# Three-block expert dispatch, spaced merges, and one layer norm moved to ScalarE

## The reference

```python
x = x + attn0(LN(x))        # q, k, v projected, each normed with gain and bias; softmax(k q^T) v + input
x = x + recur(LN(x), ctx)   # r_t = 0.9 r_(t-1) + ctx_t^2 along the sequence; LN(x) * r_t
x = x + switch(LN(x))       # top-1 of 8 experts, 256 -> 1024 -> 256 with gelu; capacity 1024 tokens, else passed by
x = x + attn1(LN(x))        # 16 heads of 16 features; q and k normed by head; softmax; projection
x = x + cross(LN(x), ctx)   # token against itself and 256 context rows, softmax
x = x + moe(LN(x))          # top-2 of 8 experts, 256 -> 256 -> 256 with relu, weighted by the raw gate scores

def moe(x, gate_w, gate_b, w1, b1, w2, b2):
    topk_s, topk_i = top_k(x @ gate_w + gate_b, 2)
    comb = zeros.at[token, topk_i].add(topk_s)
    eo = relu(x @ w1[e] + b1[e]) @ w2[e] + b2[e]      # for every expert e
    return sum_e comb[:, e] * eo[e]
```

## Time and profile before

| what | value |
|---|---|
| median of three runs | 2872.43 us |
| profiled execution | 2876.24 us, span 2874.5 us |
| granted TensorE clock, mean | 0.926 of full speed |
| stage one / switch experts | 0 to 562 / 562 to 989 us |
| attention pass / cross pass | 989 to 1938 / 1938 to 2419 us |
| expert stage | 2419 to 2874.5 us |

### The profile page before, as it was taken

The page is one execution under the profiler, slowest core; times in us unless marked ns, Lnnn a source line. Parts: engine busy times, 40 slices in busy tenths (PEclk is TensorE's granted clock), DMA queues, the critical chain, the costliest instruction groups (busy, mean ns, idle before and its releaser), DMA issues. The chain is left out here.

```text
span 2874.5 us, 49242 instructions
## 1 busy us (share of the span) xinstructions
PE 2397.5 (83%) x16164; PEld 1881.5 (65%) x16164; DVE 1971.9 (69%) x4760; ACT 1444.4 (50%) x2778; POOL 1335.4 (46%) x1248
## 2 busy tenths in 40 slices
PE   5888888579999579999999999878999885998670
PEld 3666666469999546566565665547888774997560
DVE  4888888556565357878888888745777775765563
ACT  3666666345555247777777777753444341222110
POOL 5777777544443255444344454403656553002545
PEclk9999999889999878999999999889999997999885
DMA  2222212152121000001000010003333343444665
GB/s 69 59 74 59 74 60 63 47 153 95 63 84 40 25 18 30 27 30 31 30 30 30 27 34 23 23 25 127 103 115 117 111 147 118 140 140 152 205 199 157
DMA packets 208168, 226.68 MB, mean 79 GB/s; under 512 B 32254, under 2 KB 194048, under 8 KB 207664
## 3 DMA queue, kind: packets, MB, share of 16 engines
q1 hardware_dynamic: 186352, 177.14, 19.7%
q0 software_dynamic: 20480, 46.39, 5.1%
q10 hardware_dynamic: 1088, 0.00, 0.0%
HBM read 131.99 MB, written 95.49 MB: 79 GB/s over the span
## 5 line engine op out<-in xcount | busy, mean ns | idle before, releaser
L1333 POOL TENSOR_TENSOR f_hm<-f_hm,f_mhalf 128x64 f32<-128x64 f32 x32 | 347.4, 10856 | 2.7
L1513 DVE TENSOR_REDUCE f_nm<-f_raw 128x4 f32<-128x1024 f32 x256 | 312.1, 1219 | 34.0 <-PE f_raw L1634 33.9
L1406 ACT ACTIVATE f_PT<-f_sco 128x1024 f32<-128x1024 f32 x256 | 262.7, 1026 | 81.7 <-PE f_sco L1652 78.7
L2359 POOL DMA_INDIRECT d_pick<-expert_out,e_out_slots x128 | 129.5, 1012 | 319.0 <-DMA expert_out<-d_eo 227.7
L2378 ACT ACTIVATE d_hh<-d_H 128x512 fp32r<-128x512 f32 x78 | 46.7, 598 | 283.9 <-PE d_H L2455 240.7
L1634 PE MATMUL f_raw<-f_k4T,f_q4T 64*128 64x256 f32 x1024 | 140.3, 355 | 37.5 <-DVE f_nm L1513 36.6
L895 ACT ACTIVATE b_hT<-b_H,b_b1r 128x512 f32<-128x512 f32 x128 | 88.3, 690 | 163.5 <-PE b_H L1024 148.5
L1634 PEld LDWEIGHTS f_raw<-f_k4T,f_q4T 64*128 64x128 f32 x1024 | 84.2, 203 | 105.8 <-DVE f_nm L1513 54.3
L1889 POOL DMA_INDIRECT expert_in<-g_xm,e_slots x128 | 130.9, 1023 | 39.7 <-issue 37.0
L1039 PE MATMUL b_O<-b_w2l,b_hTh 128*128 128x256 f32 x512 | 145.8, 285 | 0.0
L1039 PE MATMUL b_O<-b_w2h,b_hTh 128*128 128x256 f32 x512 | 144.8, 283 | 0.0
(11 more groups left out here) (364 smaller groups left out, 7755.6 us busy)
## 6 DMA issues: line engine op xcount, KB each, us to landing
d_xs<-expert_in SPq DMA_DIRECT2D x78, 256.0 KB
expert_out<-d_eo SPq DMA_DIRECT2D x78, 256.0 KB
x_scratch<-a_x SPq DMA_DIRECT2D x64, 256.0 KB, 2.2
b_w<-in_L_ffn_W_dram SPq DMA_DIRECT2D x16, 1024.0 KB
a_x<-in_x_dram SPq DMA_DIRECT2D x32, 256.0 KB
a_cx<-in_ctx_dram SPq DMA_DIRECT2D x32, 256.0 KB
f_x<-x_scratch SPq DMA_DIRECT2D x32, 256.0 KB
f_xr<-x_scratch SPq DMA_DIRECT2D x32, 256.0 KB
```

The lines of the kernel that those rows point to most:

```text
L1333: g.tensor_tensor(hm[b % 2][:, :], hm[b % 2][:, :], mhalf[:, :], ALU.pow).then_inc(hroot, 1)
L1406: s.activation(PT[n % 3][:, t, :, :], heads(SCO), ACT.Exp, scale=float(DH) ** -0.5).then_inc(probs_ready, 1)
L1513: v.tensor_reduce(nm[:, t, g * HG:(g + 1) * HG], heads(RAW), AX.X, ALU.max, negate=True)\
L2359: g.indirect_dma_start(pick[b % GR][:, t, c, :], None, ex.eo_d[k], bass.IndirectOffsetOnAxis(ap=ex.out_slots[:, b, t, c:c + 1], axis=0), b ...
```

## The change

Four edits.

1. In stage one the normalisation of x2 and the row that passes by are made on ScalarE, each as two ACTIVATE (scale and bias per row); the second has a part of its own, "x2 pass". GpSimd's `root4` has five small steps instead of two, since it must give -mean/std and 1 + 1/std as well, and no longer makes the sum itself. The stage's `ORDER` is rewritten.
2. `ORDER` of the attention pass is rewritten.
3. `BLOCKS` is (17, 9, 6). This makes 41 + 25 + 19 = 85 tiles, a third call of `tables` and a third `pad`.
4. GR is 4, and `ready_after` spaces merges 1.5 tiles apart: block 0's 17 after tiles 45, 46, 48, 49, ... 69, block 1's nine after tiles 70, 72, 73, ... 82, block 2's six after the last.

```diff
@@ stage one
-            "in stats", "in norm", "x2 kv", "route logits", "sco scores", "x2 sums", "x2 add", "ln sq", "in T",
-            "x2 stats", "sco exp", "route ranks", "in qk0", "ln scale", "sco prT", "in qk1", "ln kT", "x2 norm",
-            "sco inv", "sco att", "x2 T", "sco stats", "in v", "ln qT")
+            "in stats", "x2 kv", "route logits", "in norm", "sco scores", "x2 sums", "x2 add", "ln sq", "in T",
+            "x2 stats", "sco exp", "route ranks", "in qk0", "ln scale", "sco prT", "ln kT", "in qk1", "x2 norm",
+            "sco inv", "sco att", "ln qT", "x2 T", "sco stats", "x2 pass", "in v")
@@ GpSimd
             def root4(b):
                 pool.wait_ge(var4, b + 1)
-                root(rs4[b % 2][:, :], mv4[b % 2][:, :, 1], T, None, rstd4)
-
-            def passed_by(b):
-                pool.wait_ge(x2n_ready, b + 1)
-                if b >= 3:
-                    pool.wait_ge(x3_stored[b % 3], 16 * (b // 3))
-                g.tensor_tensor(x3[b % 3][:, :, :], x2[b % 3][:, :, :], x2n[b % 2][:, :, :], ALU.add).then_inc(x3_ready, 1)
+                if b >= 2:
+                    pool.wait_ge(x3_ready, b - 1)
+                stand_alone(pool, pool_passed)
+                step(g.tensor_scalar(minus4[:, :], mv4[b % 2][:, :, 0], -1.0, None, ALU.mult))
+                step(g.tensor_scalar(rs4[b % 2][:, :], mv4[b % 2][:, :, 1], EPS, None, ALU.add))
+                step(g.tensor_tensor(rs4[b % 2][:, :], rs4[b % 2][:, :], mhalf[:, 0:T], ALU.pow))
+                step(g.tensor_tensor(nmr4[b % 2][:, :], minus4[:, :], rs4[b % 2][:, :], ALU.mult))
+                g.tensor_scalar(rsp4[b % 2][:, :], rs4[b % 2][:, :], 1.0, None, ALU.add).then_inc(rstd4, 1)
@@ ScalarE
+            def norm4(b):
+                act.wait_ge(rstd4, b + 1)
+                if b >= 2:
+                    wait_full(act, "x2 T", b - 2)
+                for t in range(T):
+                    last = s.activation(x2n[b % 2][:, t, :], x2[b % 3][:, t, :], ACT.Identity,
+                                        bias=nmr4[b % 2][:, t:t + 1], scale=rs4[b % 2][:, t:t + 1])
+                last.then_inc(x2n_ready, 1)
+
+            def passed_by(b):
+                act.wait_ge(rstd4, b + 1)
+                if b >= 3:
+                    act.wait_ge(x3_stored[b % 3], 16 * (b // 3))
...
+                last.then_inc(x3_ready, 1)
@@ attention pass
-            "in stats", "raw 0", "qk scale", "att 0", "raw 1", "att 1", "out o0", "in norm", "out o1", "raw 2",
-            "att 2", "head var", "in normT", "qk gamma", "out oT", "raw 3", "att 3", "in qk0", "qk high", "in qk1",
...
+            "raw 0", "in stats", "att 0", "raw 1", "att 1", "out o0", "in norm", "out o1", "raw 2", "att 2",
+            "qk scale", "head var", "in normT", "qk gamma", "out oT", "att 3", "raw 3", "in qk0", "qk high",
...
+            "att 5", "qk split1", "qk split2", "raw 6", "qk split3", "att 6", "qk split4", "qk split5", "att 7",
+            "raw 7", "raw max1", "qk split7", "qk split6", "raw shift1", "att end")
@@ dispatch and expert stage
-        self.BLOCKS = (B - B // 3, B // 3)
+        self.BLOCKS = (B // 2 + 1, B // 4 + 1, B // 4 - 2)
-    XR, ER, GR = 6, 3, 3
+    XR, ER, GR = 6, 3, 4
-                if k + 1 < len(ex.BLOCKS):
-                    ready_after.append(first[k + 1] + 2 + b * (ex.tiles[k + 1] - 3) // n)
-                else:
-                    ready_after.append(N)
+                after = ready_after[-1] + 1.5 if ready_after else 0
+                ready_after.append(min(N, max(after, first[k] + ex.tiles[k] + 4)))
+        ready_after = [int(m) for m in ready_after]
```

More of the change, by code:

```diff
@@ L156, in phase_a @@
         x2, st4, mv4, rs4 = sbn("x2", 3, [P, T, D]), sbn("st4", 2, [P, T, 6]), sbn("mv4", 2, [P, T, 2]), sbn("rs4", 2, [P, T])
+        minus4, nmr4, rsp4 = sb("minus4", [P, T]), sbn("nmr4", 2, [P, T]), sbn("rsp4", 2, [P, T])
         x2n, x2nT, x3 = sbn("x2n", 2, [P, T, D]), sbn("x2nT", 2, [P, C, S]), sbn("x3", 3, [P, T, D])
@@ L375, in _ @@
             slots({"in stats": rstd1, "in T": residual, "ln sq": rstd2, "ln scale": gain_v, "sco stats": root3,
-                   "x2 stats": root4, "x2 T": passed_by, "route ranks": file_tokens})
+                   "x2 stats": root4, "route ranks": file_tokens})
             for u in range(FR):
@@ L444, in square_ctx @@
                 s.activation(kv[b % 2][:, :, :], cx[b % CR][:, :, :], ACT.Square).then_inc(kv_ready, 1)
+            def norm4(b):
[10 more added lines that the diff above has]
+                    act.wait_ge(x3_stored[b % 3], 16 * (b // 3))
+                for t in range(T):
+                    last = s.activation(x3[b % 3][:, t, :], x2[b % 3][:, t, :], ACT.Identity,
+                                        bias=nmr4[b % 2][:, t:t + 1], scale=rsp4[b % 2][:, t:t + 1])
+                last.then_inc(x3_ready, 1)
             def take_x2nT(b):
@@ L453, in _ @@
                    "ln qT": partial(take_T, "ln qT", qT, gqT, bqT), "ln kT": partial(take_T, "ln kT", kT, gkT, bkT),
-                   "sco exp": exps, "sco prT": take_prT, "x2 kv": square_ctx, "x2 T": take_x2nT})
+                   "sco exp": exps, "sco prT": take_prT, "x2 kv": square_ctx, "x2 norm": norm4, "x2 T": take_x2nT, "x2 pass": passed_by})
         @block.vector
@@ L547, in stats4 @@
                 dve.wait_ge(x2_ready, b + 1)
+                if b >= 2:
+                    dve.wait_ge(rstd4, b - 1)
                 row_stats(st4[b % 2], mv4[b % 2], x2[b % 3], var4)
[L550 to L555, removed]
             def step(ins):
@@ L626, in _ @@
                    "in v": take_v, "sco scores": score_max, "sco inv": invert, "sco att": attend, "sco stats": stats3,
-                   "x2 sums": recur, "x2 add": add2, "x2 stats": stats4, "x2 norm": norm4,
+                   "x2 sums": recur, "x2 add": add2, "x2 stats": stats4,
                    "route logits": route, "route ranks": queue})
```

## The result

The changed kernel takes 2891.16 us (median of 8 runs, 2880.39 to 2897.10); the kernel before takes 2868.82 (8 runs). The ratio is 1.0067, 95% interval 1.0046 to 1.0088: slower by 0.7%. I had forecast 2866 us, a small gain. The time lies in the range, but the sign was wrong, and the interval excludes it.

A forecast was written before the change was run, and what follows sets the result against it. No engine bounds the whole: stage one and attention were sums of waits, the expert stage a price per tile and merge. -25 - 10 + 8 + 20.5 = -6.5 gave 2866 us, range 2822 to 2896.

The forecast's parts named there:

- Stage one, -25: Stage one: TensorE's waits fall from 2.08 to 1.28 us a round, 0.8 over 31 rounds, -25 us.
- Attention pass, -10: Attention pass: most of TensorE's wait at the values goes, 0.32 us a round over 31 rounds, -10 us.
- fourth rival: Attention pass: shorter waits keep the clock up in all rounds, 23 us go, 2843 us; chance 0.10.
- Tables and pads, +8: Cross pass: first table -1.2, new middle table +6.2, one more pad +3, sum +8 us.
- Expert stage, +20.5: Expert stage: seven more tiles +26.6, four more merges between tiles +15.1, shorter tail -21.2, sum +20.5 us.
- 3.78 us for a merge: Expert stage: mean price above the tiles over 22 merges before, kept for the changed kernel's 26 merges between tiles.
- second rival: Merge stretch: spaced pairs cost 2.8 us more each for 13 pairs, +37, 2903 us; chance 0.18.
- The 1.6 that I had given as deciding the sign: Merge stretch: extra us a pair of merges said to decide the sign, bringing the sum from -6.5 to +14.
- signs of being wrong that I had named: Merge stretch near 5 us a tile or above 7, or stage one moving by under 10 us or over 45.
- slower: Whole kernel above 2886.8 us: chance 0.24, given as 0.18 + 0.05 + 0.01.
- third rival: Stage one: TensorE comes to wait for ScalarE, the -25 is gone, 2891 us; chance 0.09.
- first rival: Expert stage: spacing ends the pipeline's hold during gathers, a merge costs 1.75 us, stage -32, 2813 us; chance 0.20.

The follow-up runs named there:

- the second pair: Changed kernel and kernel before, both unaltered, run and profiled again: 2897.35 and 2875.29 us in the profiles' runs; changed kernel's ratio 1.0090.
- paced_third: Changed kernel with the first two blocks' gathers paced by tile counts, third run of this: 2834.95 us for 2867.68 before, ratio 0.9889.
- the three parts: Kernel before with one part each: stage one's edit (ratio 0.9962), the attention pass's order (0.9945), the blocks, ring and merge spacing (1.0044).
- blocks_only: Kernel before with only blocks of 17, 9 and 6, ring of four and merges spaced by 1.5 tiles: 2828.26 us, ratio 1.0044.

## Why the prediction was wrong

By its own steps:

1. **Stage one, -25: right in the rounds, 6 to 9 us too good in all.** The rounds gave 31 x (15.75 - 15.01) = -23. What I left out is the end: the last batches run through x2 with nothing beside them, so root, normalisation and transposes are bare there. From the last a_nm to the first output of the switch experts the changed kernel takes 4.9 us longer (4.2 in the second pair). TensorE's wait for x2n between 480 and 625 us is 8.8 us in the changed kernel; in before, between 500 and 640, it is 5.8 (8.9 and 7.4 in the second pair), so this wait is 1.5 to 3.0 of them.

```profile
PE a_bank L652 <- ACT a_x2n L453: 8.8, 2, 6.3
```

2. **Attention pass, -10: right in the mean, by a mechanism half seen.** The wait at the values went, and both kinds of round lost 0.8 us, not 0.32. But more rounds run at the lower clock: of 25 rounds 13 are the long kind in both profiles of before, 16 and 20 in the two of the changed kernel. A round averages 26.73 and 26.99 us for 27.3. The gain in this pass differs by 11 us between the two pairs, of the 18 by which the pairs differ in all; this is most of why one execution is a poor witness here. My fourth rival had the opposite: shorter waits didn't keep the clock up.

3. **Tables and pads, +8: +10.** The rounds at the new middle table are 8.6 us longer, where I had 6.2 for the table. The pad that I counted at 2.2 and more stands behind the last load of g_x (2315.10) and lengthens no round.

4. **Expert stage, +20.5: the failing step, +30 to +35.** Tiles (+26.6) and tail (-21.4 and -22.0 for -21.2) were right. The failing term is 3.78 us for a merge, carried over as a mean from before to 26 merges. Over all 26 it is 4.27, so the merges add (278.1 - 44 x 3.80) - (188.9 - 27 x 3.80) = +24.6 us where I had +15.1. In before, gathers run in eights and also in fours with a gap of a microsecond or two, since merges come one per tile: a run of twelve, six of eight and seven of four. With pairs and a free tile there are one of sixteen, ten of eight and two of four. The long runs bring tiles of 9 us and more: 8 such tiles for 22 merges in before, 12 for 26 in the changed kernel. The other tiles with a merge mostly take 5 to 7 in before and 4.9 in the changed kernel. I wrote that spacing "doesn't change the number of gathers" and stopped there; the number isn't the price. `paced_third` changes only when the gathers are issued, and halves it.

   I had the sign of this in the second rival: spaced pairs dearer than the mean. Its price was 2.8 a pair; measured it is about 1.0, (4.27 - 3.78) x 2. The 1.6 that I had given as deciding the sign is where the sum passes +14; the sum turns at 6.5 / 13 = 0.5 a pair, so this term alone turned the sign, and the shortfall of stage one brought the rest. The signs of being wrong that I had named were too coarse for this: the merge stretch came out at 278.1 / 44 = 6.3 us a tile and stage one moved by 16 to 19 us, both inside. In the chances, "slower" has at most 0.06 for the third rival, whose 2891 us lie above its bound and which had 0.09.

5. **The first rival, that the hold goes,** is false for spacing by itself, and half true for gaps between gathers. Merges that cost VectorE's time alone are what two groups of runs show (1.05 us a merge). In a group with the hold only the plain transfers and the kernel without gathers show it. The rule that the prediction quotes from the Trainium skill, "DMA never contends with a compute engine", agrees with these and not with the 84 us that the gathers cost where there is a hold.

6. **The reference value.** The forecast is set from 2872.43, the median of three runs; over eight it is 2868.82.

With the second pair the steps add up: -16.2 - 6.5 + 10.5 + 34.9 = +22.7, and the medians of the same runs differ by 25.9. What is not settled is why a group of runs has the hold or hasn't, and by what way gathers delay TensorE's results. Had the changed kernel met only runs without it, it would most likely have been faster: the three parts add up to -14 us there, and its versions with paced gathers and with a ring of three, whose stretches are the same 195 us, took 0.995 to 0.996 of before. Unaltered it wasn't run there.

## What to carry to other kernels

When a cost is read as a mean over many occurrences, look at how they are strung together before carrying it over: eight gathers in a row and the same number in threes and fives take the same time of GpSimd and don't cause the same wait. An engine's queue that runs ahead as far as its buffers allow, and has nothing urgent in it, is worth pacing by the progress of those that it disturbs. When a gain of half a per cent is at stake, take the profile of a second execution and compare by stage; here two pairs of profiles of the same kernels differed by 18 us, 11 of them in one pass.

## What the runs showed of the hardware

- GpSimd's indirect gathers (128 rows of 1 KB each, one issued every 1.31 us) delay the use of TensorE's results in some groups of runs. A merge then costs 4.09 to 4.64 us where most runs are of eight (4.27 in the changed kernel), 3.66 to 3.92 in before's mixture, 2.08 in runs of three and five, 2.17 in threes, 1.05 (VectorE's share) without gathers. Plain transfers from SyncE of the same bytes and row size hold nothing (194.6 us for 278.2, same group). Consecutive rows don't help (273.5).
- In other groups the same program has no hold, and before takes 2813 to 2815 us instead of 2868 to 2873; the 50 to 56 us lie in the one stretch. The same chip was seen in both.
- The DMA engines are busy for as long in both: 0.58 x 278.1 = 161 us in the held stretch of the changed kernel, 0.82 x 194.5 = 159 us in that of `blocks_only`. The share is 0.56 to 0.64 in held stretches with long runs of gathers and 0.81 to 0.87, at 253 to 274 GB/s, in those without the hold; so the DMA engines don't limit the held one.
- ACTIVATE of 128x256 with scale and bias per row takes 0.60 us; with a scale alone, as in the earlier trace rows, 0.50.
